# Attention scores: the mask as an additive bias, and the row maximum kept by the instruction that copies scores out of PSUM

## What is computed

```python
x = x + mixer(layernorm(x))
Q = layernorm(x) @ Wq.T + bq;  K = ctx @ Wk.T + bk;  V = ctx @ Wv.T + bv
sim = einsum('bqd,bkd->bqk', Q, K)
sim = where(mask, -1e9, sim)            # mask: (4, 512, 1601) of booleans
x = x + (softmax(sim) @ V) @ Wo.T + bo
x = x + routed_ffn(layernorm(x))
```

## Time and profile before

| what | value |
|---|---|
| median of 3 runs | 1065.64 us (1062.32 to 1066.44) |
| span of the profiled execution | 1119.2 us; no separate time is given for it |
| from its first to its last instruction | first 205 us: no attention; 205 to 720 us: attention beside scans, then alone; from 720 us: experts |
| busy: TensorE, VectorE, GpSimd, ScalarE | 908.4, 670.0, 599.3, 446.0 us |

### The profile page before, as it was taken

How to read it: one execution, slowest core, us unless ns; L and a number is a source line. 1 busy time by engine, 2 the same in 40 slices (tenths; PEclk the granted TensorE clock), 3 DMA queues, 4 the chain that set the end, 5 groups by cost and what they waited for, 6 DMA issues and landing times. The chain is left out here.

```text
span 1119.2 us, 16281 instructions
## 1 busy us (share of the span) xinstructions
PE 908.4 (81%) x5148; PEld 723.8 (65%) x5149; DVE 670.0 (60%) x1091; ACT 446.0 (40%) x827; POOL 599.3 (54%) x499
## 2 busy tenths in 40 slices
PE   5767667899969999788998779736279999999665
PEld 2344345576856677665677647735279999999564
DVE  5188789887789877876878433275034444443215
ACT  2555754467554476543555112231023333332111
POOL 2157785866666676658777132007743466425750
PEclk9989887999969999988999589957589999999686
DMA  9450020000170000530003100045513332212222
GB/s 321 157 199 1 2 113 38 1 15 1 40 264 1 16 1 2 199 103 7 9 1 110 42 7 8 20 155 191 146 39 115 115 115 75 78 37 70 61 89 90
DMA packets 48955, 85.45 MB, mean 76 GB/s; under 512 B 6292, under 2 KB 38696, under 8 KB 46856
## 3 DMA queue, kind: packets, MB, share of 16 engines
q1 hardware_dynamic: 43032, 65.77, 17.4%
q0 software_dynamic: 5872, 19.02, 5.6%
HBM read 65.64 MB, written 14.55 MB: 72 GB/s over the span
## 5 line engine op out<-in xcount | busy, mean ns | idle before, releaser
L413 POOL TENSOR_TENSOR u<-dtx,b_all 128x512 f32<-128x512 f32 x256 | 324.9, 1281 | 176.6 <-DVE h L662 172.9
L662 DVE TENSOR_TENSOR_SCAN h<-da,u 128x512 f32<-128x512 f32 x256 | 307.5, 1215 | 55.8 <-ACT da L497 33.9
L497 ACT ACTIVATE da<-dt_,a_neg 128x512 f32<-128x512 f32 x256 | 174.5, 690 | 105.9 <-DVE h L662 105.2
L785 PEld LDWEIGHTS ysum<-ident,h 128*128 128x128 f32 x1024 | 128.4, 152 | 94.5 <-DVE h L662 45.0
L785 PE MATMUL ysum<-ident,h 128*128 128x128 f32 x1024 | 157.7, 293 | 32.5 <-DVE h L662 25.5
L1421 DVE TENSOR_TENSOR hid<-act_,ps_u 128x352 f32<-128x352 f32 x78 | 40.4, 521 | 134.7 <-ACT act_ L1272 128.4
L965 PE MATMUL pv<-pT,ctx_n 128*128 128x128 f32 (+1 forms) x832 | 104.6, 276 | 1.4 <-DVE x_all L722 1.3
L965 PEld LDWEIGHTS pv<-pT,ctx_n 128*128 128x128 f32 (+1 forms) x832 | 98.4, 192 | 6.5 <-DVE x_all L722 3.2
L936 PE MATMUL pa<-ctx_t,xnT_a 128*128 128x401 f32 (+1 forms) x256 | 94.2, 502 | 3.6 <-ACT xnT_a L548 1.8
L1272 ACT ACTIVATE act_<-ps_g 128x352 f32<-128x352 f32 x78 | 36.1, 465 | 149.9 <-PE ps_u L1535 92.6
L1559 PE MATMUL ps_y<-w_hi,hidT_hi 128*128 x234 | 68.1, 291 | 19.0 <-issue 15.0
(11 more groups left out here) (217 smaller groups left out, 1796.4 us busy)
## 6 DMA issues: line engine op xcount, KB each, us to landing
b_all<-b_dram SPq DMA_DIRECT2D x16, 1024.0 KB, 4.7
ctx_t<-in_ctxT SPq DMA_DIRECT2D x4, 1601.0 KB
ctx_n<-in_ctx SPq DMA_DIRECT2D x4, 1536.0 KB
ffn_sorted<-yg SPq DMA_DIRECT2D x1, 4992.0 KB, 22.5
ffn_sorted<-y_sb SPq DMA_DIRECT2D x39, 128.0 KB
tok_in<-tok SPq DMA_DIRECT2D x35, 128.0 KB
mask<-in_mask SPq DMA_DIRECT2D x16, 200.1 KB, 2.4
w_raw<-in_w1T SPq DMA_DIRECT2D x4, 704.0 KB
```

What stands on the lines that cost most here:

```text
L413: nc.gpsimd.tensor_tensor(u[:, i % 2, :], dtx[:, j % 2, :], b_all[:, n, :], ALU.mult).then_inc(u_ok, 1)
L497: nc.scalar.activation(da[i % DS][:], dt_[:, j % 2, :], ACT.Exp, scale=a_neg[:, j, n:n + 1]).then_inc(da_ok, 1)
L662: nc.vector.tensor_tensor_scan(h[:, i % HS, :], da[i % DS][:], u[:, i % 2, :], 0.0, ALU.mult, ALU.add).then_inc(scan_ok, 1)
L785: last = nc.tensor.matmul(ysum[:, t * P:(t + 1) * P], h[:, i % HS, t * P:(t + 1) * P], ident[:], is_transpose=True, start=n == 0 and t == ...
```

## The change

The bias replaces the filled row: `sim` now holds 0 where the mask is clear and a value of about −1e9 × 2^70 where it is set, the same for every column of a row. Adding a score to it leaves that value as it is, so a row whose columns are all masked still gets equal weights. Each pick adds the chunk of scores to it, writes the sum, and carries the maximum on from the chunk before through `run_max`; the last chunk's value is that of the row. GpSimd's inversion and VectorE's reduction are gone. A pick waits for the pick before it. A mask load waits for the fill of the block two before.

```diff
+HEAVY = 2.0 ** 70
...
+        run_max = sb("run_max", [P, 2, 4])
...
                 def load_mask(b, q):
-                    wait(sp, pick_ok, b * QCH * T + QCH * (q - 1))
+                    wait(sp, fill_ok, b * T + q - 1)
...
-                                    nc.gpsimd.tensor_scalar(sim[:, q % 2, :], mask[:, q % 2, 0:S2], 0.0, neg_c[:, q:q + 1],
-                                                            ALU.mult, ALU.add).then_inc(fill_ok, 1)
-
-                                    nc.gpsimd.tensor_scalar(mask[:, q % 2, 0:S2], mask[:, q % 2, 0:S2], -1.0, 1.0,
-                                                            ALU.mult, ALU.add).then_inc(inv_ok, 1)
+                                    nc.gpsimd.tensor_scalar(sim[:, q % 2, :], mask[:, q % 2, 0:S2], neg_c[:, q:q + 1], None,
+                                                            ALU.mult).then_inc(fill_ok, 1)
...
                     dve.wait_ge(setup_ok, 6)
+                    nc.vector.tensor_scalar(neg_c0[:], neg_c0[:], HEAVY, None, ALU.mult).then_inc(setup_ok, 1)
+                    dve.wait_ge(setup_ok, 7)
...
                     if c == 0:
-                        dve.wait_ge(inv_ok, a * T + q + 1)
+                        dve.wait_ge(fill_ok, a * T + q + 1)
                     dve.wait_ge(s_mm, a * QCH * T + QCH * q + c + 1)
-                    nc.vector.copy_predicated(sim[:, q % 2, lo:hi], mask[:, q % 2, lo:hi], pa[c % 2][:, 0:hi - lo]).then_inc(pick_ok, 1)
+                    wait(dve, pick_ok, a * QCH * T + QCH * q + c)
+                    nc.vector.tensor_tensor_reduce(
+                        out=sim[:, q % 2, lo:hi], in0=pa[c % 2][:, 0:hi - lo], in1=sim[:, q % 2, lo:hi], scale=1.0,
+                        scalar=run_max[:, q % 2, c - 1:c] if c else NEG_HUGE, op0=ALU.add, op1=ALU.max,
+                        accum_out=run_max[:, q % 2, c:c + 1]).then_inc(pick_ok, 1)
 
                 def maximum(a, q):
                     dve.wait_ge(pick_ok, a * QCH * T + QCH * (q + 1))
-                    nc.vector.reduce_max(row_max[:, q:q + 1], sim[:, q % 2, :], AX_X).then_inc(max_ok, 1)
-                    dve.wait_ge(max_ok, a * T + q + 1)
-                    nc.vector.tensor_scalar(row_max[:, q:q + 1], row_max[:, q:q + 1], -1.0, None,
+                    nc.vector.tensor_scalar(row_max[:, q:q + 1], run_max[:, q % 2, QCH - 1:QCH], -1.0, None,
                                             ALU.mult).then_inc(nmax_ok, 1)
...
-                                nc.vector.tensor_scalar(neg_c[:], pv[:, 0:T], -1.0, neg_c0[:], ALU.mult,
+                                nc.vector.tensor_scalar(neg_c[:], pv[:, 0:T], -HEAVY, neg_c0[:], ALU.mult,
                                                         ALU.add).then_inc(c_ok, 1)
```

More of the change, by code:

```diff
@@ L225, in mixer_phase @@
             sem(n) for n in ("da_ok", "u_ok", "scan_ok", "sum_ok", "yT_ok", "back_mm", "y_ok", "yg_ok", "op_mm", "x1_ok"))
-        q_mm, q_ok, c_mm, c_ok, s_mm, fill_ok, inv_ok, pick_ok, max_ok, nmax_ok, exp_ok, rinv_ok = (
-            sem(n) for n in ("q_mm", "q_ok", "c_mm", "c_ok", "s_mm", "fill_ok", "inv_ok", "pick_ok", "max_ok",
+        q_mm, q_ok, c_mm, c_ok, s_mm, fill_ok, pick_ok, nmax_ok, exp_ok, rinv_ok = (
+            sem(n) for n in ("q_mm", "q_ok", "c_mm", "c_ok", "s_mm", "fill_ok", "pick_ok",
                              "nmax_ok", "exp_ok", "rinv_ok"))
```

## The result

The changed kernel takes 1073.33 us (median of 7 runs, 1071.71 to 1076.26) where the kernel before takes 1065.64 us beside it: a ratio of 1.0077, 95% interval 1.0056 to 1.0098, so slower by about 8 us. The prediction was 1064.6 us with a range up to 1069, and "same".

A forecast was written before the change was run, and what follows sets the result against it. TensorE's ordered stream was taken as the bound wherever changed instructions run; steady −0.4, last batch 0.0 and drain −0.4, about −1 us together, took 1065.64 to 1064.6 us, with a range of 1058 to 1069 us.

The forecast's parts named there:

- the term for the fill: GpSimd in attention: 16 fills stay at 1.607 us each, with one arithmetic step less; only the inversions go (25.4 us).
- Two signs named beforehand: Steady batches: a TensorE gap waiting for `sim` means wrong; picks starting 154 to 155 us apart mean right.
- The sum beside that term: Mixer, 205 to 720 us: steady −0.4, last batch 0.0, drain −0.4, together about −1 us.
- The pick: VectorE, 64 picks: 0.80 us each with accumulator read, 0.20 more than now, bounded by 0.57 and 1.14 us.
- The added wait: VectorE: each pick waits for the pick before it; costed at nothing, covered by the spacing between picks.
- the 0.2 us gap: Steady batch, TensorE waiting for a scan at 244.65 us: freed by the removed inversion, twice 0.2 us.
- the 0.8 us for `dtx`: Steady batch, a TensorE wait for VectorE: not counted as gained, since inputs before it come from TensorE.
- The last batch: Last batch with scans: gaps freed −0.6 and −0.2, longer picks +1.0, removed reductions −0.2, together 0.0 us.
- Rival 1: Mixer: freed VectorE and GpSimd time closes TensorE's gaps, 7.4 us in all, giving 1058.2 us; chance 0.21.
- Rival 2: Attention: the new pick runs at the scan's rate, 1.14 us, costing +5.5 us, 1071.1 us; chance 0.10.
- Rival 3: Attention: the maximum merely moves and TensorE hides every pick's effect, 1065.6 us; chance 0.10.
- The bound: Wherever changed instructions run, TensorE's ordered stream bounds; freed VectorE or GpSimd time counts only in TensorE's idle gaps.

The follow-up runs named there:

- two_steps: Changed kernel with GpSimd's fill given a second arithmetic step that does nothing (plus 0.0): 1116.10 us beside 1119.55 for the kernel before, ratio 0.9966.
- both_two_steps: two_steps with the same do-nothing step added where GpSimd scales expert outputs (line 1254 of the kernel before): ratio 0.9967 to the kernel before.
- add_then_max: Kernel with the bias and two-step fill, but picks by plain addition and the reduction over 1601 columns back: ratio 0.9980 to the kernel before.
- fill_on_scalar: Changed kernel with the fill moved from GpSimd to ScalarE: ratio 1.0011 to the kernel before.

## Why the prediction was wrong

**The step that failed** is the term for the fill: "the 16 fills of 1.607 us stay, with one arithmetic step less and the same elements". I had taken the fill over at the old duration, as if fewer steps could only be as fast or faster, without bounding it, though the trace of before held no one-step instruction of this size. It did hold one of the same form: line 1254, 0.925 us for 256 elements, more than half of the 1.607 us that the fill took for 1601. Divided by elements, 3.6 against 1.0 ns, this would have been the warning, and an upper bound of 5.8 us for the fill. With the fill at its true length, 4.332 us, the time is 14.2 us longer than with a fill of 1.603 us (+10.4 against −3.8 us), in the direction opposite to all the small terms. Two signs named beforehand showed it: a gap on TensorE in the steady batch for a pick (1.6 us), and a second steady batch that picks 156.9 us after the first instead of 154 to 155.

**The sum beside that term** had the right sign and was too small: −1 us forecast, −3.8 measured with the fill at 1.6 us (on the 1065.64 us level 1062.0, within my range).
- The pick: 0.80 us taken, 0.705 measured. The bounds 0.57 and 1.14 held. The trace shows two instructions where one was before. "VectorE: DVE Perf Modes" of the Trainium skill, "Two Vector instructions with no wait between them", says this of an operation that writes out its accumulator, and the trace agrees. The read is 0.083 us, half of what I had taken. The main part, 0.622 us, is close to the pointer-scalar form's 0.63 and far from the scan's rate, 0.95. VectorE's busy time fell by 21 us in the changed kernel, where I had expected 14 to 18.
- The added wait cost nothing that any row shows.
- Steady batch: the 0.2 us gap went, as foreseen, and the 0.8 us for `dtx` stayed in two of the three profiles with this mixer.
- The gaps: from the first attention to the last TensorE is idle 49.7 us in `two_steps` and 50.2 before. The last batch had 0.0 in my sum, and the second steady batch 0.2. Where the 3.8 us of `two_steps` lie can't be read from single executions: it has 3.5 of its 4.0 us in the second steady batch and `both_two_steps`, the same kernel up to the experts, 6.7 of its 8.0 us in the last (the table above). Much of this is the clock. Windows over the same 3 us of before, `two_steps` and `both_two_steps` (stretch, length, busy us of PE, PEld, DVE, ACT and POOL with instructions, granted clock, DMA share, GB/s):

```profile
511.00:514.00 3.00, 3.00 (x12) 2.48 (x13) 0.87 (x1) 0.00 (x0) 3.00 (x4) 0.50 0.00 0
```

```profile
511.00:514.00 3.00, 3.00 (x14) 1.80 (x14) 0.34 (x2) 0.00 (x0) 3.00 (x5) 1.00 0.00 0
```

```profile
511.00:514.00 3.00, 3.00 (x7) 1.66 (x7) 1.94 (x3) 0.00 (x0) 2.10 (x3) 0.50 0.00 0
```

After a wait for `xn` TensorE is at half its clock here in the first and third, and at its full 2.4 GHz in the second, though the second and third run the same instructions. From the transposition behind that wait to the first score chunk TensorE needs 13.5, 10.3 and 13.4 us in the three. In the last batch the two transpositions of `xn` lie 28.2 us apart in `two_steps` and 23.6 in `both_two_steps`, with the same waits between them. So how long the clock stays down after a wait differs from one execution to the next, and several microseconds of a trace's distances are that. Where the 3.8 us of the timed runs come from stays open.

**The rivals.** Rival 1 (faster through closed gaps): once the fill is mended, half of its 7.4 us is there, but not its mechanism. From 458 to 592 us TensorE waits 1.7 us for a scan, 1.4 for picks and 0.7 for `x_all` in `two_steps`, against 1.9, 1.2 and 0.8 before. Rival 2 (slower) had the right side and the wrong place: the pick is not slow, but an instruction whose new form I had not measured is. Rival 3 is refuted by `two_steps` and `add_then_max`. The upper end of the range, 1069 us, was said to be half of the way to rival 2; half of the way is 1067.9 us, and neither reaches the measured time.

**The bound.** "What VectorE or GpSimd gives back is worth time only where TensorE sits idle for them" holds for what is given back: in `two_steps` VectorE and GpSimd are busy 19 and 20 us less from the first attention to the last, and TensorE's idle time is 49.7 us against 50.2. I had drawn no conclusion for what is added. The step from 6.2 to 8.7 us of GpSimd at the first two blocks costs TensorE a wait of 1.6 us, and of the doubled reductions a third reaches the time: the slack behind TensorE is small.

**The port.** The `dt_` addition that falls beside a fill took 3.17 us in the changed kernel, where its usual length is 0.69 and its longest was 1.58 before:

```profile
240.49 3.17 DVE L627 TENSOR_TENSOR dt_<-sp_pos,dt_ 128x512 f32<-128x512 f32 x1 [1.21 <-ACT dt_ L468]
```

The fill ran from 239.78 to 244.11 us. With a fill of 1.60 us beside it the addition took 1.43 us (`two_steps`), and with the fill on ScalarE 0.69 us (`fill_on_scalar`):

```profile
240.78 1.43 DVE L626 TENSOR_TENSOR dt_<-sp_pos,dt_ 128x512 f32<-128x512 f32 x1 [1.21 <-ACT dt_ L467]
```

```profile
239.26 0.69 DVE L625 TENSOR_TENSOR dt_<-sp_pos,dt_ 128x512 f32<-128x512 f32 x1 [1.21 <-ACT dt_ L456]
```

So it is GpSimd's fill that holds it up. "SBUF — State Buffer" of the Trainium skill, "Who interferes with whom", says that a VectorE instruction with two SBUF inputs contends with a GpSimd instruction that reads SBUF, and the traces agree. The addition ended 0.45 us before the fill did, though, so the trace doesn't show a lock held to the very end of GpSimd's instruction; beside the two-step fill it ended 0.54 us behind.

## What to carry to other kernels

An edit that makes an instruction do less is a new instruction: look for a row of exactly its form, on its engine, and divide by the elements, before taking over the old duration. Where a second engine runs close behind the bound, removed and added time are not worth the same; ask of each term which way it pushes. A single profile can't place a few microseconds where the clock moves: compare the same stretch in two executions first. When a slow form is found, try the fast form with a step that does nothing.

## What the runs showed of the hardware

- GpSimd's `tensor_scalar` with one arithmetic step costs about 1.7 ns more per element than with two: 4.33 against 1.60 us for 1601 elements from bytes to f32, 4.26 with a constant, and 0.925 against 0.480 us for 256 elements of f32.
- VectorE's addition with a running maximum over 401 columns, one input in PSUM, took 0.575 us with a constant start and 0.622 us with the start read from SBUF; the accumulator read behind it took 0.083 us.
- The length of a low-clock stretch after a wait differed between executions of the same instructions: from 511 to 514 us granted 1.00 in one kernel and 0.50 in another with the same mixer, and the same matmuls took 10.3 and 13.4 us.
- A wait of 6.06 us on TensorE, inside a stretch that had been at full clock, was followed by a granted clock of 0.56 over 6 us, and matmuls of 1.6 us took 3.0.
- VectorE's addition of two 128x512 tiles in SBUF took 0.69 us with no fill beside it, 1.43 beside a GpSimd instruction of 1.60 us and 3.17 beside one of 4.33 us.
